# First image's halo in smaller pieces on two queues, and the transposes of two images placed later, in a chain of convolutions and an expert MLP

## What is computed

```python
def _gn(v, G=4, eps=1e-05):
    g = v.reshape(B_, G, C_ // G, H_, W_)
    m = jnp.mean(g, axis=(2, 3, 4), keepdims=True)
    s = jnp.var(g, axis=(2, 3, 4), keepdims=True)
    return ((g - m) / jnp.sqrt(s + eps)).reshape(v.shape)
...
x = x + _L0_conv_ref(_gn(x), L0_conv_weight, L0_conv_bias)
x = x + _L1_conv_ref(_gn(x), L1_conv_weight, L1_conv_bias)
x = x + _L2_conv_ref(_gn(x), L2_conv_w1, L2_conv_b1, L2_conv_w2, L2_conv_b2)
x = x + _L3_conv_ref(_gn(x), L3_conv_weight, L3_conv_bias)
```

## Time and profile before

| what | us |
|---|---|
| median of three runs | 595.76 |
| lowest and highest | 594.5 and 597.54 |
| the profiled execution | 597.69 |
| its span in the trace | 595.9 |
| steps 0 to 5, first small matmul to the wait of step 6 | 37.89 to 107.8 |
| steps 6 and 7 to the first MLP matmul | 111.45 to 150.04 |
| the MLP, expert 0's second half to the last | 184.29 to 493 |

### The profile page before, as it was taken

How to read it: one execution, slowest core, us unless ns; L and a number is a source line. 1 busy time by engine, 2 the same in 40 slices (tenths; PEclk the granted TensorE clock), 3 DMA queues, 4 the chain that set the end, 5 groups by cost and what they waited for, 6 DMA issues and landing times.

```text
span 595.9 us, 9048 instructions
## 1 busy us (share of the span) xinstructions
PE 532.5 (89%) x3326; PEld 260.9 (44%) x3326; DVE 366.1 (61%) x648; ACT 273.1 (46%) x318; POOL 160.3 (27%) x169
## 2 busy tenths in 40 slices
PE   1679999796989999999999999999999988786956
PEld 1335445353544444444444444444444445443422
DVE  4669999599676394292490670851933396867323
ACT  2797788223535453362451551633533364455600
POOL 4597888733360000000000000000000012575600
PEclk9869999799799999999999999999999997768998
DMA  8655555521120121012101101210100000323695
GB/s 331 273 129 137 145 135 147 147 73 71 70 71 1 70 72 71 2 68 70 70 0 70 70 21 49 70 70 0 70 0 1 0 2 1 101 70 92 241 312 172
DMA packets 12725, 53.18 MB, mean 89 GB/s; under 512 B 2956, under 2 KB 3084, under 8 KB 9356
## 3 DMA queue, kind: packets, MB, share of 16 engines
q1 hardware_dynamic: 11532, 45.88, 24.6%
q10 hardware_dynamic: 1164, 6.91, 3.0%
HBM read 25.83 MB, written 8.39 MB: 57 GB/s over the span
## 4 chain that ended last, share of the span: by engine, by line
PE 72%; DVE 14%; POOL 4%; DMA 3%; SPq 3%; ACT 3%; issue 2%; DVEq 0%; POOLq 0%; ACTq 0%
PE PS L915 28%; PE PS L894 26%; PE PS L804 7%; PE PS L797 7%; DVE ST L578 5%; DVE X L617 3%; SPq L248 3%; DVE X L633 3%; DMA X<-x 1%; DMA HALO<-XN 1%; POOL XN L342 1%; PE PS L855 1%; DVE XT L626 1%; ACT SCR L426 1%; PE PS L871 1%
## 5 line engine op out<-in xcount | busy, mean ns | idle before, releaser
L894 PE MATMUL PS<-XT,W1S 128*128 (+1 forms) x768 | 171.7, 382 | 7.0 <-DVE W1S L640 6.8
L915 PE MATMUL PS<-HID,W2S 128*128 128x512 f16 x768 | 172.6, 383 | 1.6 <-DVE W2S L640 1.6
L458 ACT ACTIVATE SCR<-PS,CONST 128x512 f32<-128x512 f32 x128 | 87.2, 687 | 75.0 <-PE PS L894 38.8
L894 PEld LDWEIGHTS PS<-XT,W1S 128*128 128x128 f16 x768 | 75.4, 99 | 96.0 <-issue 9.9
L915 PEld LDWEIGHTS PS<-HID,W2S 128*128 128x128 f16 x768 | 75.8, 99 | 89.1 <-issue 3.5
L342 POOL TENSOR_TENSOR XN<-SCR,XN 128x1024 f16<-128x1024 f32 (+1 forms) x49 | 99.2, 2031 | 23.6 <-ACT SCR L426 23.6
L691 DVE SCALAR_TENSOR_TENSOR HID<-SCR,HID 128x512 f16<-128x512 f32 x128 | 88.5, 691 | 14.1 <-ACT HID L479 10.0
L640 DVE SCALAR_TENSOR_TENSOR W2S<-W2F,W2S 128x2048 f16<-128x2048 f32 x8 | 18.3, 2290 | 118.6 <-ACT W2S L454 118.6
L315 POOL MEMSET HALO<- 48x520 f16 x12 | 6.3, 527 | 311.8 <-PE PS L894 311.3
L578 DVE BATCH_NORM_STATS2 ST<-X 128x6 f32<-128x512 f32 x128 | 81.5, 682 | 9.3 <-DMA X<-x 8.2
L421 ACT ACTIVATE XN<-X,SC 128x1024 f16<-128x1024 f32 (+1 forms) x49 | 59.6, 1215 | 53.9 <-POOL SC L333 53.9
(11 more groups left out here) (44 smaller groups left out, 405.5 us busy)
## 6 DMA issues: line engine op xcount, KB each, us to landing
W1F<-w SPq DMA_DIRECT2D x8, 1024.0 KB, 4.8
W2F<-w SPq DMA_DIRECT2D x8, 1024.0 KB, 4.8
HALO<-XN SPq DMA_DIRECT2D x48, 129.9 KB
out<-X ACTq DMA_DIRECT2D x6, 1024.0 KB, 6.3
HALO<-XN SPq DMA_DIRECT2D x48, 121.8 KB
X<-x SPq DMA_DIRECT2D x2, 2048.0 KB, 19.2
HALO<-XN SPq DMA_DIRECT2D x48, 64.9 KB
HALO<-XN SPq DMA_DIRECT2D x48, 60.9 KB
```

The source lines that it names most:

```text
L458: act.activation(SCR[:, ft % 2, 0:CH], bank(ft % G_RING), ACT.Gelu, bias=BT[:, ds(e * FT + ft, 1)], scale=1.0 / (XS * WS)).then_inc(gelu_o ...
L894: mm = pe.matmul(bank(ft % G_RING), W1S[:, w, h * NF + ft * P:h * NF + (ft + 1) * P], rhs, start=(n == 0), stop=(n == 3 * DH - 1))
L915: mm = pe.matmul(bank(G2_BANK + h), W2S[:, w, ft * NW + h * P:ft * NW + (h + 1) * P], HID[p][:, part, ft], start=(ft == 0 and part == 0 an ...
```

## The change

It has five parts.

1. `pieces(0)` becomes six pieces: chunks 4 and 5 are one each instead of one piece of two. POOL does four pieces ahead of `scale_and_bias(1)` instead of three.
2. The four thirds of step 0's first half are issued by ACT, between its fifth and sixth piece. The halo code is rewritten as `halo_columns` and `halo_thirds`; on SP the order is now four columns, then four thirds.
3. At the start, statistic 1's group sums and fillers stand behind the second centre instead of the fourth; those of statistic 2 stay behind the fourth.
4. Transposes 0 to 15 follow the table `PREPARED`: none ahead of step 6's first `tiles`, and four at the end of step 7.
5. DVE's `split_low` of the first weights stands in the middle of step 7, and ACT's `split_high` comes behind `xt_high(9)` instead of `xt_high(13)`.

```diff
+THIRDS_BY_ACT = ((0, 0),)
...
-        return [(0, 1), (1, 1), (2, 2), (4, 2), (6, 2)]
+        return [(0, 1), (1, 1), (2, 2), (4, 1), (5, 1), (6, 2)]
...
-PREPARED_AT = 6
+PREPARED = {(6, 0, 1): (0, 1), (6, QUAD, 0): (2, 3), (6, QUAD, 1): (4, 5),
+            (7, 0, 0): (6, 7), (7, 0, 1): (8, 9), (7, QUAD, 0): (10, 11),
+            (7, QUAD, 1): (12, 13, 14, 15)}
...
+    def neighbours(t0, t1):
+
+        return ((0, R - 1, -1, max(t0, 1), t1), (1, 0, 1, t0, min(t1, NT - 1)))
+
+    def halo_columns(queue, s, t0, t1, signal):
+
+        for below, row, by, u0, u1 in neighbours(t0, t1):
+            for half in range(2):
+                shifted_rows(queue, s, half * HALF_P + (BELOW if below else ABOVE),
+                             slice(row, P, R), by, u0, u1 - u0, 0, signal)
+
+    def halo_thirds(queue, s, t0, t1, signal):
+
+        for below, row, by, u0, u1 in neighbours(t0, t1):
+            for half in range(2):
+                w = 1 - half
+                shifted_rows(queue, s, half * HALF_P + THIRD + DEAL * NC * below,
+                             slice(w * HALF_P + row, (w + 1) * HALF_P, R),
+                             by, u0, u1 - u0, -1 if w == 1 else 1, signal)
...
-            halo_part(s, 0, NT // 2, halo_a[s])
+            halo_columns(sp, s, 0, NT // 2, halo_a[s])
+            if (g, 0) not in THIRDS_BY_ACT:
+                halo_thirds(sp, s, 0, NT // 2, halo_a[s])
...
-        low_parts(0, 0, 3)
+        low_parts(0, 0, 4)
         scale_and_bias(1)
-        low_parts(0, 3)
+        low_parts(0, 4)
...
-        for g in range(8):
+        slot_free(0)
+        for k in range(5):
+            normalise_piece(k)
+        act.wait_ge(lo_ok, PIECE_OF[0, QUAD] + 1)
+        halo_thirds(act, 0, 0, NT // 2, halo_a[0])
+        normalise_piece(5)
+        for g in range(1, 8):
             normalise(g)
-        for k in range(NCH):
-            xt_high(k)
-        for k in range(NPR):
-            xt_high(NCH + 2 * k)
-            xt_high(NCH + 2 * k + 1)
-            if k == 2:
+        for m in range(2 * NCH):
+            xt_high(m)
+            if m == NCH + 1:
                 split_high(W1F, W1S, w1_in, w1_hi, 0)
...
-                if g >= PREPARED_AT:
-                    xt_low(m + 2)
-                    xt_low(m + 3)
+                for m in PREPARED.get((g, i, 1), ()):
+                    xt_low(m)
                 for k in range(QUAD):
                     conv_stats(g, i + k)
                 if i == 0:
                     deviation(3 + g)
-            if g == 7:
-                split_low(W1F, W1S, w1_in, w1_hi, w1_ok, 0)
+                if (g, i) == (7, 0):
+                    split_low(W1F, W1S, w1_in, w1_hi, w1_ok, 0)
...
                 for k in range(QUAD):
                     centre(g, i + k)
-                if (g, i) == (0, 0):
-                    for n in (1, 2):
-                        group_mean(n)
-                        group_variance(n)
+                    if (g, i, k) in ((0, 0, 1), (0, 0, 3)):
+                        group_mean((k + 1) // 2)
+                        group_variance((k + 1) // 2)
```

More of the change, by code:

```diff
@@ L225, in bass_program, with shifted_rows @@
     ty_mm = sem("ty_mm")
+    def shifted_rows(queue, s, rows, src_rows, by, t0, nt, shift, signal):
+        run = (nt - 1) * PITCH + NJ
+        src = XN[s][src_rows].rearrange("p k t j -> p k (t j)")
+        n = src.shape[0]
+        dst = HALO[s][rows:rows + DEAL * (n - 1) + 1:DEAL].rearrange("p k t j -> p k (t j)")
+        f = (t0 + by) * PITCH + 1 + shift
+        queue.dma_start(dst[:, :, t0 * PITCH:t0 * PITCH + run], src[:, :, f:f + run]
+                        ).then_inc(signal, 16)
+    def neighbours(t0, t1):
[12 more added lines that the diff above has]
+                             by, u0, u1 - u0, -1 if w == 1 else 1, signal)
     block = ctx.enter_context(nc.Block())
@@ L240, in _ @@
         load_image(3, 0, NT, x3_in)
-        def shifted_rows(s, rows, src_rows, by, t0, nt, shift, signal):
-            run = (nt - 1) * PITCH + NJ
-            src = XN[s][src_rows].rearrange("p k t j -> p k (t j)")
-            n = src.shape[0]
-            dst = HALO[s][rows:rows + DEAL * (n - 1) + 1:DEAL].rearrange("p k t j -> p k (t j)")
-            f = (t0 + by) * PITCH + 1 + shift
-            sp.dma_start(dst[:, :, t0 * PITCH:t0 * PITCH + run], src[:, :, f:f + run]
-                         ).then_inc(signal, 16)
-        def halo_part(s, t0, t1, signal):
-            for below in range(2):
-                row = 0 if below else R - 1
-                u0, u1 = (t0, min(t1, NT - 1)) if below else (max(t0, 1), t1)
-                by = 1 if below else -1
-                for half in range(2):
-                    shifted_rows(s, half * HALF_P + (BELOW if below else ABOVE),
-                                 slice(row, P, R), by, u0, u1 - u0, 0, signal)
-                for half in range(2):
-                    w = 1 - half
-                    shifted_rows(s, half * HALF_P + THIRD + DEAL * NC * below,
-                                 slice(w * HALF_P + row, (w + 1) * HALF_P, R),
-                                 by, u0, u1 - u0, -1 if w == 1 else 1, signal)
         def halos(g):
@@ L661, in _ @@
             for i in range(0, NCH, QUAD):
-                m = NCH * (g - PREPARED_AT) + i
-                if g >= PREPARED_AT:
+                for m in PREPARED.get((g, i, 0), ()):
                     xt_low(m)
-                    xt_low(m + 1)
                 for k in range(QUAD):
```

14 lines of the change are left out of this document (6 added, 8 removed).

## The result

The changed kernel takes 586.02 us (median of 4 runs, 585.36 to 587.37), the kernel before on the same chip 596.23 (4 runs, 594.5 to 597.54). The ratio is 0.983, with a 95% interval of 0.980 to 0.987. The forecast was 585.3. The profiled execution took 587.37, of which the span is 585.4; before it was 597.69 and 595.9, so the traces to be compared lie 10.5 us apart. Both traces are a little slower than their medians, which lie 10.2 apart.

What follows compares the result with a forecast made beforehand. PE, busy 89% of the span, was taken to bound the kernel, with gains only where it waits or runs at its low clock. 3.3 + 7.2 = 10.5 off the median 595.76 gave 585.3; range 582.0 to 589.5.

Steps and rivals of the forecast that it cites:

- Part A: At the start, step 0's tiles begin earlier; gain 3.3 us, between 2.0 and 3.7.
- Part B: In steps 6 and 7, tiles run at once and the first MLP matmul comes earlier; gain 7.2 us.
- rival one: At the start, ACT's issues cost more than SP's; at 1.6 us each the start gains nothing, 588.6; chance 0.11.
- rival three: At the four issues at 24.9, ACT is held by its own transfers; at 3.76 us each, 597.2; chance 0.02.
- the cap: At step 1, ACT's issues delay POOL and the halo lands at 47.6, so tiles move by 3.7 us at most.
- either value: Step 0's tiles start at 35.6 if DVE's small operation waits for POOL, 33.8 if it slips in ahead.
- The two readings of `L611`: Before step 0's tiles, DVE's small operation waits for POOL twice: statistic 1 done at 23.8, `group_variance(2)` at 32.1.
- the slack grows: After step 1, SP needs 10.9 us a step and PE 11.3, so the slack grows.
- Rival two: In steps 6 and 7, PE's clock falls and tiles run slowly, 2.6 us per twelve groups; 588 to 589.5; chance 0.09.

Runs made afterwards that it cites:

- a_only: The changed kernel with transposes 0 to 15 and `split_low` placed as before, keeping the smaller pieces, ACT's thirds and nearer sums; 593.43 us.
- thirds_sp: The changed kernel with all eight transfers of the first halo issued by SP again, none by ACT; 585.34 us.
- fill35: Against thirds_sp, three fillers behind statistic 1's sums and five behind statistic 2's in place of seven and seven; 584.41 us.
- act_both: The changed kernel with the thirds of step 0's second half issued by ACT too; 589.73 us.

## Why the prediction was right, and where it was not

**The sum.** Forecast 3.3 + 7.2 = 10.5; measured 2.72 + 7.11 = 9.83, and 0.66 behind the first MLP matmul, where the same code scatters by more than that. That the span came out exactly as said, 585.4, is luck in this 0.66. Part A's 2.72 lies within its bounds of 2.0 and 3.7, and the same start gave 3.33 in a_only, so by the scatter of 0.9 either side of the 3.3 was possible.

**Part B** held step by step. The tiles of step 6 follow the centres, the weights' transfer is hidden, the transposes 14 and 15 are handed on at granted clock 0.50 (138 to 140), and the last `xt_low` releases the MLP at 140.21, within the 139 to 141. The term was 7.2 and measured 7.11, alone 7.37.

**POOL and the queues.** The single-chunk piece ends at 21.66 + 3.14 = 24.80, forecast 24.9; ACT's four issues take 2.81 us, 0.70 each, forecast 0.68. So rival one, at 1.6 an issue, and rival three, which decides from 3.4 on, fell on that one row. But the forecast stopped at the price of an issue. That ACT's issues would delay POOL was in the text, as the reason for the cap; that the part loses more by it than it gains was not, and thirds_sp showed it.

**The first tiles** came at 31.88, earlier than either value (33.8 and 35.6), and outside the 33.8 to 35.7 that the prediction named as its sign. The failed step was the clock in PE's line: I ran the centres and both sets of fillers at the low level and gave the clock back only to the tiles. It rose during the centres, so `group_mean(2)` stood at 29.16 instead of 29.9, `L611` slipped in 0.4 us ahead of POOL, and the second fillers took 1.70 instead of 3.0. The two readings of `L611` were right for the first time it meets POOL (end forecast 23.8, measured 23.73) and wrong for the second, by that margin. The Trainium skill, "SBUF — State Buffer", section "Who interferes with whom", says that a VectorE instruction with two inputs in SBUF contends with a GpSimd instruction that reads SBUF. The traces here agree: the operation took 0.22 us without POOL and 0.28 to 2.17 beside it, and ended with POOL's instruction.

**The cap.** Step 1's tiles start at 47.46, at the landing of their halo (forecast 47.6), and gain 3.87 (forecast at most 3.7). There the forecast said that the slack grows. It does not for the next half: its tiles come at 53.75 against 56.92, which is 3.17, with a halo wait of 0.63, and the meeting of `L611` and POOL at 54.79 takes 0.46 more. SP issued that half's eight transfers from 45.6 to 50.2, no slower than forecast, but PE's tiles start 3.6 us after the last issue, where the first half's landing took 2.45. That is 2.7, the mis-sized term: I took the gain at the first wait that caps it and not at the last, and counted the SBUF rule only for the two small operations in front of step 0's tiles, not for those behind.

**Rival two** was seen as a mechanism in other places (fill35, act_both) and was absent where I put it: steps 6 and 7 ran their tiles at the high clock. Its price was added up wrong: at 2.6 us a half, one or two slow halves leave B at 4.6 or 2.0, not at 3 to 4.5, and two would have been 590.5, beyond the range. The six chances of the prediction also add up to 1.01.
